# Distance tables read back in blocks of 16 rows instead of 32

## The reference, cut to what matters

```python
scores = jnp.einsum('bhqd,bhkd->bhqk', q, k) / scale
rel = build_relative_position(S, S, BUCKETS, MAX_REL)      # log buckets of q - k
c2p_att = jnp.einsum('bhqd,hpd->bhqp', q, pos_k)
c2p = jnp.take_along_axis(c2p_att, clip(rel + ATT_SPAN, 0, 2 * ATT_SPAN - 1), axis=-1)
p2c_att = jnp.einsum('bhkd,hpd->bhkp', k, pos_k)
p2c = jnp.take_along_axis(p2c_att, clip(-rel + ATT_SPAN, 0, 2 * ATT_SPAN - 1), axis=-1)
scores = scores + (c2p + swapaxes(p2c, -1, -2)) / scale
probs = jax.nn.softmax(scores, axis=-1)
```

## Time and profile before

| | |
|---|---|
| Time before, median of 3 runs | 2987.88 us (2982.29 to 2990.0) |
| The profiled execution, its time | 2991.43 us |
| The profiled execution, its span | 2989.8 us |
| PE busy | 1991.2 us, 67% |
| DVE busy | 1922.3 us, 64% |
| ACT busy | 1235.4 us, 41% |
| POOL busy | 982.9 us, 33% |
| Mean granted clock of TensorE | 0.839 |
| Transfers | 492.60 MB in 208340 packets |

### The profile page before, as it was taken

How to read it: one execution, slowest core, us unless ns; L and a number is a source line. 1 busy time by engine, 2 the same in 40 slices (tenths; PEclk the granted TensorE clock), 3 DMA queues, 4 the chain that set the end, 5 groups by cost and what they waited for, 6 DMA issues and landing times. The chain is left out here.

```text
span 2989.8 us, 48888 instructions
## 1 busy us (share of the span) xinstructions
PE 1991.2 (67%) x13524; PEld 1444.4 (48%) x13525; DVE 1922.3 (64%) x4329; ACT 1235.4 (41%) x2141; POOL 982.9 (33%) x1369
## 2 busy tenths in 40 slices
PE   4452777777777777777727888676326059999852
PEld 2221555655555656566625656544226016766421
DVE  4552788878787878788846666258846754434344
ACT  2332666666666666666612232242101063333100
POOL 3222222222222222222231221036760005555576
PEclk8775899989899989999968999887655559999976
DMA  4766998988888889898841120000001224444333
GB/s 138 210 203 201 287 288 280 281 272 277 283 284 274 276 263 287 272 289 272 270 140 38 47 57 0 20 1 0 0 0 59 97 86 128 134 130 130 100 112 106
DMA packets 208340, 492.60 MB, mean 165 GB/s; under 512 B 39168, under 2 KB 104352, under 8 KB 208128
## 3 DMA queue, kind: packets, MB, share of 16 engines
q1 hardware_dynamic: 179392, 420.25, 44.7%
q0 software_dynamic: 24576, 57.11, 7.1%
q10 hardware_dynamic: 4160, 12.58, 1.1%
HBM read 248.45 MB, written 241.30 MB: 164 GB/s over the span
## 5 line engine op out<-in xcount | busy, mean ns | idle before, releaser
L816 DVE CUSTOM_DVE_ANT_0 probs<-bank,c2p 128x512 f32<-128x512 f32 x512 | 553.2, 1080 | 228.2 <-PE bank L711 155.4
L789 ACT COPY a_stage<-bank 128x320 f32<-128x320 f32 (+1 forms) x512 | 365.3, 714 | 276.1 <-PE bank L679 255.9
L773 ACT ACTIVATE probs<-probs,neg_max 128x512 f32<-128x512 f32 x512 | 363.2, 709 | 22.8 <-DVE neg_max L816 22.3
L825 DVE COPY probsT<-bank 128x512 f32<-128x512 f32 x512 | 352.9, 690 | 2.6 <-PE bank L721 2.6
L692 PE MATMUL bank<-tab,k 96*128 96x320 bf16 (+1 forms) x512 | 162.2, 317 | 282.0 <-DVE b_stage L767 222.5
L721 PE MATMUL bank<-ident,probs 128*128 128x128 f32 x2048 | 330.4, 286 | 4.2 <-ACT probs L773 4.1
L721 PEld LDWEIGHTS bank<-ident,probs 128*128 128x128 f32 x2048 | 264.7, 150 | 18.9 <-issue 6.0
L711 PE MATMUL bank<-ident,p2c 128*128 128x128 f32 x1280 | 266.4, 310 | 0.0
L655 POOL COPY end_c2p<-a_stage 128x4 f32<-128x4 f32 (+1 forms) x128 | 24.1, 188 | 719.3 <-ACT a_stage L789 571.6
L767 ACT COPY b_stage<-bank 128x288 f32<-128x288 f32 (+1 forms) x256 | 186.7, 729 | 148.5 <-PE bank L692 147.0
L692 PEld LDWEIGHTS bank<-tab,k 96*128 96x128 bf16 x512 | 51.4, 100 | 347.2 <-DVE b_stage L767 281.7
(11 more groups left out here) (254 smaller groups left out, 3965.3 us busy)
## 6 DMA issues: line engine op xcount, KB each, us to landing
p2c_d<-b_stage SPq DMA_DIRECT2D x64, 640.0 KB, 3.7
c2p_d<-a_stage SPq DMA_DIRECT2D x64, 640.0 KB, 3.0
p2c_d<-b_stage SPq DMA_DIRECT2D x64, 576.0 KB, 7.8
c2p_d<-a_stage SPq DMA_DIRECT2D x64, 576.0 KB, 6.0
p2c<-p2c_d SPq DMA_DIRECT2D x256, 144.0 KB
c2p<-c2p_d SPq DMA_DIRECT2D x256, 144.0 KB, 6.0
o_sorted_d<-p_o_pair SPq DMA_DIRECT2D x80, 256.0 KB
q_stack_d<-p_parts SPq DMA_DIRECT2D x96, 128.0 KB
```

The costliest lines, as they stand in the source:

```text
L773: act.activation(probs[:, w % 2, j, :], probs[:, w % 2, j, :], ACT.Exp, bias=neg_max[:, w % 2, j:j + 1], scale=-1.0).then_inc(exp_done, 1)
L789: act.copy(a_stage[:, wa % 2, x0:x1, j], bank[A_BANK][:, x0:x1]).then_inc(a_copied, 1)
L816: dve.tensor_tensor_reduce(probs[:, w % 2, j, :], bank[S_BANKS[(HB * w + j) % 3]][:], c2p[:, w % 2, :, j], -SCALE, LOWEST, ALU.add, ALU.mi ...
L825: dve.tensor_copy(probsT[:, wp % 2, j], bank[T_BANKS[j % 2]][:].rearrange("p (k q) -> p k q", k=TPB)).then_inc(probsT_copied, 1)
```

## The change

`ROWS` goes from 32 to 16. `TABLE` follows, from 320 to 288 columns, and with it the width of both tables on every engine and in DRAM. A block that is read back has 16 rows of 272 columns, and eight blocks make a table instead of four. The columns that POOL fills grow by 16 on each side. The semaphore counts follow, from 64 for each table to 128.

```diff
-ROWS = 32
+ROWS = 16
 FIRST_X, TABLE = P - ROWS, 2 * P + 2 * ROWS
...
-                            wait_count(sp, p2c_loaded[wb % TPB], 64 * (4 * ib + wb // TPB))
+                            wait_count(sp, p2c_loaded[wb % TPB], P // ROWS * 16 * (4 * ib + wb // TPB))
...
-                                pe.wait_ge(p2c_loaded[kt], 64 * (4 * i + g + 1))
+                                pe.wait_ge(p2c_loaded[kt], P // ROWS * 16 * (4 * i + g + 1))
...
-                                    dve.wait_ge(c2p_loaded[w % 2], 64 * (8 * i + w // 2 + 1))
+                                    dve.wait_ge(c2p_loaded[w % 2], P // ROWS * 16 * (8 * i + w // 2 + 1))
```

## The result

| | before | after |
|---|---|---|
| Median of the runs | 2987.15 us | 3247.02 us |
| Ratio, 95% interval | | 1.087 (1.0845 to 1.0896) |
| Span of the profiled execution | 2989.8 us | 3250.5 us |
| Mean granted clock of TensorE | 0.839 | 0.805 |

I had forecast 3111 us, a range of 3030 to 3220, and slower. The direction held. The time lies above the range and the change is 2.1 times what I summed up.

The account below looks back on a forecast made before the run. No engine was full; SP's issue stream (9.6 to 10.5 us after the change) and the read-back loop (9.85 to 10.5) were to set the unit. Taken at 10.35 us, +123 us over 128 units: 3111 us, range 3030 to 3220.

Parts of the forecast that it names:

- What bounds the kernel: First attention, 9.39 us a unit: no engine full, read-backs arrive at the limit, about one unit in four waits for them.
- two loops: First attention: SP's own instruction stream must fit in a unit; table copies through read-backs to DVE take 8.0 us a unit.
- signs: First attention: stage about 1325 us, issues near 0.42 us, SP's waits for ACT under 1 us, DMA share under 0.8.
- Eight more issues: SP's stream: added read-back issues cost 3.4 to 4.3 us a unit, making SP's stream the period at 9.6 to 10.5 us.
- The sum: First attention: SP's stream and the read-backs' loop together give 10.35 us a unit, +0.96 us, or +123 us over 128 units.
- the spare time covers it: Rival, SP's stream: full-queue stalls vanish with a slower rhythm, SP in use 9.0 us; 0 to +15 us, chance 0.08.
- The cover: SP's stream: 3.2 us of waits in each unit stand against the added issues and are used up.
- The read-back loop: From table copies through read-backs to DVE, over two units: sixteen issues raise it to 9.85 to 10.5 us a unit.
- Fewer bytes: DMA engines: 5.6% less moved in a mean unit, worth between nothing and 0.45 us a unit; taken as nothing.
- narrower copies: DVE and ACT table copies: 0.07 and some 0.3 us saved a unit, only about 0.1 us in the loop.
- bytes decide: Rival, DMA engines: draining queued transfers sets most units, so 5.6% fewer bytes give -40 us, 2948 us; chance 0.05.
- it feeds on itself: Rival: PE's waits lower its clock, or stalls grow with the number of transfers; 11.3 us a unit, 3233 us, chance 0.15.

Follow-up runs that it names:

- e6: The changed kernel with both table writes cut to 16 columns from the second pass on, same count of issues; 3138.8 us, ratio 1.0504.
- e10_four_last: The kernel before with four more transfers of 16 rows with 16 bytes in each unit, issued after both read-back bursts; 3055.5 us, ratio 1.0221.
- e10_four_between: The kernel before with four more transfers of 16 rows with 16 bytes in each unit, issued between the p2c and c2p bursts; 3094.3 us, ratio 1.0351.
- e12_before_moved: The kernel before with the write of table a issued between the p2c and c2p bursts of the next step; 3044.8 us, ratio 1.0184.
- e2: The kernel before with tables of 288 columns and rows of 272, still read in four blocks of 32 rows; 2978.3 us, ratio 0.9969.
- e10_eight_last: The kernel before with eight added transfers of 16 rows with 16 bytes in each unit, behind both read-back bursts; 3253.0 us, ratio 1.0882.
- e7: c2p read-backs issued by POOL instead of SP: on the changed kernel 3186.5 us, on the kernel before 3083.2 us.

## Why the prediction was right or wrong

*What bounds the kernel* was read rightly: SP's waits as its spare time, and two loops. Of what I named as signs, most came: an issue kept its 0.42 us, SP's waits fell under 1 us for a unit, DVE's waits for c2p rose from 59 to 272 us and were its largest, the DMA share fell under 0.8. The length of the stage (1325 us forecast, 1452 measured) did not.

*Eight more issues: the term that was mis-sized.* I priced them at 3.4 to 4.3 us, with stalls of 0.6 us for a unit carried over from the profile of before. SP's time in use went from 6.2 to 11.35 - 0.3 = 11.05 us, 4.85 us more: half a microsecond above my upper bound. Of this 2.75 are in the p2c issues, 1.6 in those of c2p, 0.4 in the gaps between instructions and 0.15 in the stops at the turn of the loop. Without stalls the same eight would have been 3.7 us. The remaining 1.15 are three things: the stall behind the writes, from 0.34 to 1.06 us; the long issues that go along with instruction packets, from 0.35 to 0.60 us; and the turns, 0.15 us. I had seen stalled bursts but not asked what they stood behind, nor what the change does to it: once SP has no waits, the writes of a step come right ahead of the next burst, and each stall is paid. e6 shows it by making the writes thin. The turns go with the length of SP's stream: every run that gives SP more issues than before has long turns on SP (2.5 to 5.3 us), and none of the others has.

*The sum.* Even my own upper end for SP's stream was 10.5 us, a floor without any wait. I took 10.35 as a value near the top of both ranges; their lower ends, 9.6 and 9.85 us, had no added stall at all. The measured unit is 11.35: 11.05 in use, 0.3 of waits. The stops at the turns are 20 us of the 250 in the stage, less what the burst behind each of them gains by not being stalled. The rest of the 260 us is about 10 us outside the stage, 3 before and 7 behind it; this was not looked into.

*The rival "the spare time covers it"* took the stalls of before to come from full queues that would empty with a slower rhythm. The stalls grew instead, and e6 has 510 rows waiting and no stall.

*The cover.* I said that the added issues first use up 3.2 us of waits. As a balance for a full stream this holds. As cover it does not: 1.9 us of added issues cost 0.5 us for a unit (e10_four_last).

*The read-back loop* was put at 9.85 to 10.5 us. It is real (e10_four_between, e12_before_moved), at about a third to all of what I had worked out, but in the changed kernel the stream is longer and sets the period. Landings of c2p were 1.2 us shorter than I kept in it.

*Fewer bytes, narrower copies*: taken at nothing, measured at 10 us (e2), 0.3%. Small as I said, for the DMA engines were not the limit. The rival that bytes decide, and with it the rule of the Trainium skill (page "DMA: Bandwidth & Descriptors", section "Issuing engines are not separate DMA queues") that the sequencer's time is usually small relative to the transfer, did not hold here in the sense that counts for a full stream: the 0.42 us of an issue stand beside 0.25 us of all DMA engines for 68 KB, and sixteen bytes a row cost as much as a whole row (e10_eight_last). Beside the 2.3 us that a read-back of c2p takes from issue to landing the issue is still small.

*The rival "it feeds on itself"* gave 3233 us, 14 us from the measured time, and I cut it off at 3220. It had two reasons. The clock is not the one: the granted clock did fall, from 0.92 to 0.83 in the stretch shown, but SP, which sets the period, hardly waits for PE or what follows it. That it fell because PE idles more is likely and was not shown. The other reason, stalls that grow, was right, though not with the number of transfers as I wrote: the greater part grew behind the full-width writes, a smaller part along with instruction packets. That its number lay so near is luck: the 11.3 us for a unit was not summed from terms.

## What to carry to other kernels

Count the issues of a queue's engine as work of that engine: here 0.46 us each for blocks of 16 or 32 rows, so a transfer under about 130 KB at this stage's 278 GB/s takes more of SP's time than of the DMA engines'. Before a stream is filled up, look at what its longest instructions stand behind, and price them for the order in which they will stand when the waits between them are gone. A mean of waits is a budget, not cover: four small issues inside it cost 65 us. And look at the turn of the loop on any engine whose stream gets longer: it can go from 0.2 to 4 us.

## What the runs showed of the hardware

An issue takes SP 0.42 us in a burst whether it moves 16 rows of 16 bytes (eight in 3.54 us) or of 4352 bytes (eight in 3.59 us). Right behind the writes of both tables it took up to 2.1 us (changed kernel, at 1350.5 us). With the writes cut to 16 columns, and rows and transfers left as they were, the stall of the three issues behind them fell from 1.06 to 0.03 us for a unit. Loads of 1152 KB ahead of a burst, without full-width writes, held nothing: 0.42 us an issue. I had expected a queue that fills by count, and some 510 rows outstanding did not fill it. How the full-width writes come to hold SP, the runs don't show. A second kind of long issue, up to 2.5 us, starts within 0.4 us of a 16 KB packet of the instruction queue: all 50 issues over 1.2 us in e6_thin_writes, 48 of 75 in the changed kernel.

The turn of a loop took 0.20 to 0.23 us on SP where it has 19 instructions for a unit (before, e2, e12), and 2.5 to 5.3 us in every run where it has 23 or more; on POOL it took 0.20 to 0.23 us before and 2.8 to 4.9 us once POOL had the c2p issues too (both e7 runs). Nothing in these turns is a wait that the profile names.
